# Where one chunk's stores are issued: from ScalarE's queue to SyncE's, in a pairwise-interaction tower

## The reference

```python
e = jnp.stack([tbl_0[ids[:, 0]], ..., tbl_38[ids[:, 38]]], axis=1)      # 512 x 39 x 16
x0 = xk = e
for idx, (W, b) in enumerate([(w0, b0), (w1, b1), (w2, b2)]):
    z = relu(jnp.einsum('bhd,bkd,hks->bsd', x0, xk, W) + b[None, :, None])   # 128 outputs
    if idx != 2:
        xk = z[:, :64, :]; direct.append(z[:, 64:, :])
    else:
        direct.append(z)
z = jnp.sum(jnp.concatenate(direct, axis=1), axis=-1)                   # 512 x 256
h = jnp.concatenate([z, dense_ctx], axis=1)
y = relu(relu(h @ W_top1 + b_top1) @ W_top2 + b_top2) @ W_top3
```

## Time and profile before

| | us |
|---|---|
| three runs of the kernel before | 660.06, 661.51, 1059.06; median 661.51 |
| the profiled execution | 660.79 |
| its span, first to last instruction | 658.8 |
| start of chunk 0's first L1 product | 52.79 |
| length of step 2 (L0 of chunk 2 to L0 of chunk 3) | 36.34 |

### The profile page before, as it was taken

One profiled execution on the slowest core, in us unless ns is written; L12 is line 12 of the kernel. 1 busy time (PEld: TensorE's weight loads), 2 busy tenths in 40 slices (PEclk: granted clock), 3 DMA queues, 4 the chain that ended last, 5 costly groups with the idle time before them and its releaser, 6 DMA issues. The chain is left out here.

```text
span 658.8 us, 6297 instructions
## 1 busy us (share of the span) xinstructions
PE 610.5 (93%) x2000; PEld 375.5 (57%) x2000; DVE 558.9 (85%) x632; ACT 408.2 (62%) x550; POOL 536.6 (81%) x325
## 2 busy tenths in 40 slices
PE   4137989999999999999999999999999999999998
PEld 1014546666666665666656665656666566665553
DVE  2327889898989989898989899898989898988971
ACT  2005576667585867766675857676676758575632
POOL 6755889898989989898989999898989896865540
PEclk9976999999999999999999999999999999999999
DMA  6678473655556584736464564737364645620000
GB/s 224 155 173 253 109 210 67 187 120 136 143 122 203 139 250 76 240 77 206 96 182 101 138 187 90 235 77 237 78 200 96 180 110 128 193 64 1 0 0 0
DMA packets 64043, 90.29 MB, mean 137 GB/s; under 512 B 46624, under 2 KB 49568, under 8 KB 60042
## 3 DMA queue, kind: packets, MB, share of 16 engines
q1 hardware_dynamic: 54334, 85.25, 47.1%
q0 software_dynamic: 5120, 1.29, 2.1%
q10 hardware_dynamic: 4556, 3.35, 1.8%
HBM read 87.31 MB, written 8.95 MB: 146 GB/s over the span
## 5 line engine op out<-in xcount | busy, mean ns | idle before, releaser
L385 POOL TENSOR_TENSOR low<-prod,high 128x1024 fp32r<-128x1024 f32 (+1 forms) x160 | 381.0, 2399 | 63.1 <-ACT high L474 60.3
L648 DVE TENSOR_TENSOR prod<-spread,x 128x1024 f32<-128x1024 f32 x256 | 308.1, 1214 | 42.1 <-issue 15.8
L756 PE MATMUL z<-prod,w_sb 128*128 128x512 f32 (+2 forms) x608 | 290.7, 598 | 30.3 <-DVE prod L648 15.4
L474 ACT ACTIVATE high<-prod 128x1024 fp32r<-128x1024 f32 (+1 forms) x160 | 167.9, 1058 | 119.6 <-DVE prod L648 98.0
L773 PE MATMUL z<-high,high_w_L 128*128 128x512 f32 (+1 forms) x448 | 203.0, 453 | 4.4 <-ACT high L484 2.6
L788 PE MATMUL z<-low,high_w_L 128*128 128x512 f32 (+1 forms) x448 | 181.9, 487 | 3.9 <-POOL low L385 2.4
L375 POOL DMA_INDIRECT gat<-table_dram,index x160 | 154.9, 968 | 36.5 <-issue 34.2
L756 PEld LDWEIGHTS z<-prod,w_sb 128*128 128x128 f32 (+2 forms) x608 | 115.8, 191 | 117.0 <-issue 86.6
L773 PE MATMUL z<-high,low_w_L 128*128 128x512 f32 (+1 forms) x448 | 177.9, 397 | 0.0
L788 PEld LDWEIGHTS z<-low,high_w_L 128*128 128x128 f32 (+1 forms) x448 | 82.1, 189 | 69.8 <-issue 45.7
L494 ACT ACTIVATE x<-z,bias_sb 64x512 f32<-64x512 f32 (+1 forms) x174 | 112.5, 646 | 14.0 <-PE z L756 7.4
(11 more groups left out here) (37 smaller groups left out, 89.2 us busy)
## 6 DMA issues: line engine op xcount, KB each, us to landing
spread<-x_rows SPq DMA_DIRECT2D x14, 1792.0 KB
spread<-x_rows SPq DMA_DIRECT2D x32, 768.0 KB, 13.3
spread<-x_rows SPq DMA_DIRECT2D x16, 1024.0 KB
x_rows<-x_rows SPq DMA_DIRECT2D x15, 390.0 KB
x0base<-x_rows SPq DMA_DIRECT2D x44, 78.0 KB
gat<-table_dram,index POOLq DMA_INDIRECT x160
x_rows<-gat SPq DMA_DIRECT2D x29, 72.0 KB
spread<-x_rows ACTq DMA_DIRECT2D x1, 1792.0 KB
```

What stands on the lines that cost most here:

```text
L385: pool.tensor_tensor(low[0:rows, h, 0:k, :], prod[0:rows, slot(c, kind, g), 0:k, :], high[0:rows, h, 0:k, :].bitcast(F32), ALU.subtract).t ...
L474: act.activation(high[0:rows, split_slot(c, kind, g), 0:k, :], prod[0:rows, slot(c, kind, g), 0:k, :], ACT.Copy).then_inc(high_ready, 1)
L648: dve.tensor_tensor(prod[0:rows, slot(c, kind, g), :, :], spread[0:rows, c % 2, g, :].unsqueeze(1).to_broadcast([rows, k, N]), x[0:rows, : ...
L756: last = pe.matmul(z[:, :], w[0:rows, at + j, :], prod[0:rows, slot(c, kind, g), j, :], start=g == 0 and j == 0, stop=closes and j == k - 1)
```

## The change

Chunk 1's stores, its `x0base` loads and its `spread0` load move from ScalarE's program to SP's. On SP's queue the stores stand between chunk 0's repeat and chunk 0's three pieces; the `x0base` and `spread0` loads stand between chunk 0's pieces and chunk 1's pieces. ScalarE keeps chunk 1's repeat, which now stands behind the relu copies. `load_second` is gone, and ScalarE's `store_x0` becomes `store_again`, which issues the same two DMAs of chunk 0 as before. Nothing else changes: the same DMAs with the same sizes, the same arithmetic.

```diff
@@ -341,8 +341,11 @@
             for n, (at, end) in enumerate(FIRST_CUTS):
                 load_first(at, end, spread0_first[n], (0, 1))
             repeat_x0(0)
+            store_x0(1)
             for p in range(len(PIECES)):
                 load_spread(0, p)
+            load_base(1)
+            load_spread0(1)
             for p in range(len(PIECES)):
                 load_spread(1, p)
             store_x0(2)
@@ -410,17 +413,15 @@
-            def store_x0(c, copies):
-
-                act.wait_ge(gathered[c], 16 * GAT)
-                for n in copies:
...
+            def store_again():
+
+                act.wait_ge(gathered[0], 16 * GAT)
...
@@ -430,18 +431,6 @@
-            def load_second():
-
-                for j in range(DPT):
-                    row = x0_dram[1, (F - j * T0) % F:(F - j * T0) % F + 1, 0:1]
-                    act.dma_start(x0base[j * F:(j + 1) * F, :], bass.AP(row.tensor, row.offset, [[N, F], [1, N]])
-                                  ).then_inc(base_in, 16)
-                act.wait_ge(prod_done, PROD_NUMBER[0, "L0", G0 - 1])
-                act.wait_ge(x0_copied[1], 16)
-                row = x0_dram[1, 0:1, 0:1]
-                act.dma_start(spread0[:, :, :].rearrange("p t n -> p (t n)"),
-                              bass.AP(row.tensor, row.offset, [[N, P], [1, T0 * N]])).then_inc(spread0_in, 16)
@@ -550,7 +539,7 @@
-            store_x0(0, (1,))
+            store_again()
             load_first()
             take_base(0)
@@ -584,11 +573,9 @@
                     if kind == "L0" and i == 0:
-                        store_x0(1, (0, 1))
-                        repeat_second()
                         shared_copies(0, x1, z0, "L0", 0, x1_ready)
                         relu0(i, 2)
-                        load_second()
+                        repeat_second()
             relu2(NCH - 1)
```

More of the change, by code:

```diff
@@ L411, in split_weights @@
                                ).then_inc(high_w_ready, 1)
-            def store_x0(c, copies):
-                act.wait_ge(gathered[c], 16 * GAT)
-                for n in copies:
[L417 to L423, removed]
+            def store_again():
+                act.wait_ge(gathered[0], 16 * GAT)
+                first = x0_dram[0, F:F + 1, 0:1]
+                act.dma_start(bass.AP(first.tensor, first.offset, [[D, P], [FPT * N, GAT - 1], [1, D]]),
+                              gat[:, 0, 0:GAT - 1, :]).then_inc(x0_stored[0], 16)
+                tail = x0_dram[0, F + FPT * (GAT - 1):F + FPT * (GAT - 1) + 1, 0:1]
+                act.dma_start(bass.AP(tail.tensor, tail.offset, [[D, LAST], [1, D]]),
+                              gat[0:LAST, 0, GAT - 1, :]).then_inc(x0_stored[0], 16)
             def repeat_second():
```

## The result

| | before | changed |
|---|---|---|
| runs | 660.06, 661.51, 662.03 | 651.25, 651.47, 652.32, 653.21 |
| median, us | 661.51 | 651.89 |
| profiled execution, us | 660.79 | 651.47 |
| its span, us | 658.8 | 649.7 |

The ratio of the times is 0.9862, with a 95% interval of 0.9834 to 0.9890: 1.4% less, within 2% and well clear of no change. A fourth run of the kernel before took 1059.06 us and isn't counted here. The changed kernel was run twice more beside the kernel before, with ratios of 0.9858 and 0.9890, so its gain is 1.1 to 1.4%. The profiled execution is 9.3 us shorter where 10.4 were forecast; its span is 9.1 us shorter.

What follows compares the result with a forecast made beforehand. Full steps have no room (TensorE busy 36.21 of 36.34 us in step 2), so gains lie ahead of them. L1 10.6 us earlier less 0.2 gives 10.4 off 660.8: 650.4 us, range 649.0 to 655.5.

Steps and rivals of the forecast that it cites:

- The bound and the passage to the end: Full steps have no room; time gained ahead of the steady part passes to the end one for one, step 2 unchanged.
- The relu copies: Behind chunk 0's L0: ScalarE's copies start at 38.74 like VectorE's, whose half ends last, at 41.87.
- The stores and the issue of the pieces: On SP's queue: chunk 1's stores issued 34.05 to 36.19, landed by 39.4; chunk 0's pieces issued from 36.2, 2.5 us later.
- The first piece: Chunk 0's 768 KB load: through at 40.9, usable at 41.6 with 0.7 us completion; L1 starts at 42.2, 10.6 us earlier.
- the second piece: Chunk 0's load, first used 3.0 us into L1: usable at 44.9, needed at 45.2, margin 0.3 us; 0.2 us charged.
- the first rival: Loads become the next wait, chunk 0's first piece or chunk 1's `spread0`: 2 to 4.4 us lost, 652.5 to 655; chance 0.17.
- Chunk 1's repeat and `spread0`: Ahead of chunk 1's L0: repeat issued at 42.1, done at 50.1; `spread0` landed at 56.7, needed at 58.2, no cost.
- The second rival: ScalarE still held at its repeat ahead of L1's `take_high`, by late stores or a blocked issue: 654.1 to 655.9; chance 0.10.
- The rule on queues: Skill's rule that all issuers' DMAs interleave on 16 engines; by it chunk 1's stores would stay slow on SP's queue.

Runs made afterwards that it cites:

- four-piece kernel: Changed kernel with spread loaded in four pieces (512, 512, 768, 768 KB) instead of three; 650.18 us, ratio 0.9842; run again 651.48 us, 0.9851.
- stores on ScalarE: Changed kernel with chunk 1's stores issued by ScalarE again, behind L0's `take_high`, the repeat still behind the relu copies; 656.74 us, ratio 0.9914.
- stores behind the pieces: Changed kernel with chunk 1's stores on SP's queue behind chunk 0's pieces instead of ahead; 657.48 us, ratio 0.9941.
- loads left on ScalarE: Changed kernel with chunk 1's `x0base` and `spread0` loads put back on ScalarE, behind its repeat; 658.63 us, ratio 0.9945.
- split kernel: Changed kernel with one of the two copies of chunk 1's stores issued by ScalarE ahead of the relu copies, the other by SP; 651.85 us, ratio 0.9859.
- kernel with the loads alone: Kernel before with only chunk 1's `x0base` and `spread0` loads moved to SP's queue, between chunk 0's and chunk 1's pieces; 661.76 us, ratio 0.9997.
- stores doubled: Changed kernel with chunk 1's two store copies issued once more into a spare DRAM buffer, ahead of the real ones on SP's queue; 656.33 us, ratio 0.9910.
- kernel with both edits: Changed kernel with one store copy of chunk 1 issued by ScalarE and spread loaded in four pieces; 650.13 us, ratio 0.9839.
- kernel with the stores behind and the repeat on SP: Changed kernel with chunk 1's stores behind chunk 0's pieces and its repeat behind them, all on SP, no repeat on ScalarE; 653.46 us, ratio 0.9872.

## Why the prediction was right, point by point

**The bound and the passage to the end: right.** Step 2 is 36.34 us long in both, and the 9.06 us at chunk 1's L0 are the 9.1 of the span.

**The relu copies: right.** They begin at 38.80 behind L0's sum; VectorE's end last, at 42.01 (forecast 41.87).

**The stores and the issue of the pieces: right.** First issue 34.25 (34.05), pieces at 36.44 (36.2). The stores had landed by 38.82, when the repeat's wait was passed, sooner than the 39.4 of the forecast. The repeat itself went out at 38.82 and not at 42.1: I had put it behind the end of the relu copies, but ScalarE issued it while the first copy ran. In the kernel before the same can be seen, the issue at 53.14 ahead of the end of the work in front of it. What that was worth is said under chunk 1's repeat.

**The first piece: the term that was mis-sized.** I had put first data at 37.5, 3.4 us for 768 KB and 0.7 us for completion, 41.6, ahead of the copies' end; it was used at 43.31. The table of stretches of the changed kernel has the pieces' first bytes at 217 GB/s:

```profile
35.00:37.50 2.50, 2.50 (x7) 1.32 (x7) 0.00 (x0) 0.00 (x0) 2.04 (x3) 1.00 0.57 64
37.50:41.00 3.50, 1.27 (x4) 0.38 (x2) 2.06 (x3) 2.12 (x4) 2.58 (x4) 1.00 0.96 217
41.00:45.00 4.00, 0.42 (x1) 0.42 (x2) 2.66 (x4) 1.14 (x2) 2.73 (x3) 0.68 1.01 231
```

3.5 us x 217 GB/s are 0.76 MB, so the bytes of a first piece (0.79 MB) have moved by about 41.1. The transfer was sized rightly; the 0.7 us behind it were 2.2. The trace's single DMA packets tell where most of it goes: of the 16 engines' completion marks of this piece, thirteen fall between 40.5 and 41.4 and three at 42.34 to 42.36. VectorE started 0.95 us behind the last of them, at 43.31, and not behind the thirteenth. The four-piece kernel agrees: a first piece of two thirds of the size removes the wait. This cost 1.1 us of start (9.48 earlier instead of 10.6), and the second piece another 0.33 where I had charged 0.2. Together that is the difference between the forecast and what was measured (10.4 us against 9.06 at chunk 1's L0, 9.1 in the span and 9.3 in the time), and it was named as the first rival, if with a smaller price than there (2 to 4.4 us).

**Chunk 1's repeat and `spread0`: right in the outcome.** `x0_copied[1]` came at 51.88 (50.1), `spread0` was no wait: L616 was released by `base`, as before. The repeat came 1.7 us later than forecast, and its 13.1 us from issue are near the upper bound of 13.8 that I had given it. The margin that I had put at 1.5 us was about 0.9, an estimate: where `spread0` was the wait it was used 7.0 us behind its issue, which makes 58.9 here, against 59.78. So the forecast of no cost held with little to spare. Whether it helped that the repeat was issued 3.3 us sooner than I had assumed is open: no packet of it moved before 45.0.

**The second rival didn't happen here, and the runs show that it was no phantom.** ScalarE held between L0 and L1 costs 5 to 6.7 us (stores on ScalarE, stores behind the pieces, loads left on ScalarE). Against these times, 656.74 to 658.63, even the upper end of the prices that I gave it, 654.1 to 655.9, was 0.8 to 2.7 us too low. Two things are shown to be needed to keep it away: the stores ahead of the pieces, and the loads off ScalarE. That the repeat must stand behind the copies is not shown; no run has early stores with the repeat still ahead of the copies. In the second execution of the changed kernel ScalarE reached the copies at 37.63 and the repeat left at 38.48, 3.97 us behind the first store issue. By that, an estimate, the stores of the first had landed at about 38.2, ahead of L0's sum at 38.80. With the repeat ahead of them the copies would then have ended by about 42, before the first piece at 43.31, so with early stores this part of the edit may be worth nothing.

**The rule on queues.** Behind the pieces the stores are as slow on SP's queue (first issue 36.61, landed by 50.85, 14.2 us) as on ScalarE's (34.05 to 49.16, 15.1 us), and ahead of them they are fast: 34.25 to at most 38.82 on SP's, and 34.89 to at most 38.98 in the split kernel, where half of them is on ScalarE's. The order against the pieces matters, and the queue doesn't. The Trainium skill, "DMA: Bandwidth & Descriptors", section "Issuing engines are not separate DMA queues", says that DMAs of all issuing engines run on the same 16 DMA engines and interleave. For the stores the traces agree in that the other queue saves nothing but the issue on ScalarE. That two queues always interleave they don't show; the last section has 6 us in which they didn't.

## What to carry to other kernels

A wait in an engine's program holds the compute behind it too; look at each DMA issue on a computing engine for what it waits for, and when that comes, and move the waiting ones behind the work that others wait for or to an engine that only issues. When the longest of several waits in a row is removed, the next ones come to light: here two parts of the edit, one worth nothing alone (the loads) and one that makes chunk 0's pieces late (the stores ahead of them), keep the gain from being given back. Small stores behind large loads took three times as long as ahead of them; ahead, they cost the loads their issue time and a little more.

## What the runs showed of the hardware that I had not expected

**A DMA on an idle queue can stand still behind another queue's.** The changed kernel's repeat was issued on ScalarE's queue (q10) at 38.82, while SP's queue (q1) had its three pieces. The page of the DMA queues over 39 to 45 us names q1 and q0 only, and over 45 to 52 also q10 with all of the repeat (queue, packets, MB, share):

```profile
q1 hardware_dynamic: 249, 1.38, 100.1%
q0 software_dynamic: 36, 0.01, 1.1%
```

```profile
q1 hardware_dynamic: 293, 1.20, 61.0%
q10 hardware_dynamic: 208, 0.40, 21.3%
```

For 6 us no packet of the repeat moved, so here the two queues didn't take turns. The blocked issues of small stores (6.22 us before, 6.00 with the stores on ScalarE, 4.24 in the kernel with the loads alone, 5.16 and 4.90 with them behind the pieces on SP's own queue, 5.01 and 4.95 with the repeat there too) fall into the stretches in which the same pieces move, and in each the pieces had been issued before the blocked one. That one limit on issued but unmoved work, common to both queues, lies behind all of these was not tested.

**TensorE's clock fell a second time in some executions.** In the changed kernel's profile the granted clock is 0.50 in chunk 0's gap (42.4 to 49.2, against 42.4 to 59.4 before), and 1.00 from there on. In the split kernel it fell again within step 1. The same stretch in the split and in the changed kernel:

```profile
82.40:85.80 3.40, 3.40 (x7) 1.38 (x5) 3.37 (x5) 0.98 (x2) 3.25 (x3) 0.50 1.03 340
```

```profile
82.40:85.80 3.40, 3.40 (x12) 2.12 (x12) 3.37 (x5) 1.24 (x2) 3.24 (x3) 1.00 0.96 331
```

TensorE was busy throughout in both, and the trace has 7 matmuls of it in the one and 12 in the other. Step 1 became 39.78 us instead of 38.32, also with the stores doubled (103.69 - 63.92 = 39.77), where the clock was 0.50 from 86.8 to 90.2. Ahead of both falls, and in the changed kernel without one, TensorE has gaps: it is busy for 2.74 of 4 us from 80 to 84 in the split kernel (the largest gap is a wait of 1.26 us for GpSimd's low part), for 2.73 in the changed one, so nearly the same work can get either clock. How often it happens can't be read from the mean clock of an execution. All four of the split kernel had 0.992, and of the changed kernel's twelve six had 0.992 and six 0.995, but one of these six, the second profiled one, has no second fall; its first low stretch lasted 10.3 us (40.2 to 50.5) instead of 6.8, and its step 1 took 38.30 us. Whether the split brings the fall on or met it by chance is open. In the kernel with both edits the clock fell at 67.8 to 71.2 and step 1 kept its 38.31 us, as it did in the kernel with the stores behind and the repeat on SP (65.0 to 68.4, 38.32 us). So a fall early in step 1 cost nothing, and one late in it 1.45 us. It is of the size of the gains that the last edits were after.
